# A layer of causal attention and soft mixture of experts in five stages: rows kept in SBUF for the slots stage, first inputs fetched a stage ahead, last stores awaited by their readers

## The reference, cut to what matters

```python
x = _layernorm(x + attention(x))          # causal, 16 heads of 32, 4 key/value groups
x = _layernorm(x + ffn(x))
# ffn, a soft mixture of E = 16 experts with S = 128 slots each:
x_ln = layernorm(x) * gamma + beta
x_n = l2norm(x_ln) * scale;  mu_n = l2norm(mu, 0)
logits = einsum('bnd,des->bnes', x_n, mu_n)
dispatch = softmax(logits, axis=1)                          # over tokens
combine = softmax(logits.reshape(B, N, E * S), axis=-1)     # over all slots
slot_in = einsum('bnd,bnes->besd', x_ln, dispatch)
slot_out = gelu(slot_in @ W1 + b1) @ W2 + b2
out = einsum('bsd,bns->bnd', slot_out, combine)
```

## Time and profile before

| what | value |
|---|---|
| time of the runs, median | 2615.83 us |
| time of the profiled execution | 2613.21 us |
| its span | 2611.5 us |
| granted TensorE clock, mean | 0.967 |
| PE busy | 2472.7 us, 95% |
| DVE busy | 1745.1 us, 67% |
| POOL busy | 1637.5 us, 63% |
| ACT busy | 1447.1 us, 55% |
| bytes moved by DMA | 337.98 MB |

### The profile page before, as it was taken

The page is one execution under the profiler, slowest core; times in us unless marked ns, Lnnn a source line. Parts: engine busy times, 40 slices in busy tenths (PEclk is TensorE's granted clock), DMA queues, the critical chain, the costliest instruction groups (busy, mean ns, idle before and its releaser), DMA issues. The chain is left out here.

```text
span 2611.5 us, 39531 instructions
## 1 busy us (share of the span) xinstructions
PE 2472.7 (95%) x13218; PEld 1725.6 (66%) x13218; DVE 1745.1 (67%) x3729; ACT 1447.1 (55%) x2780; POOL 1637.5 (63%) x1681
## 2 busy tenths in 40 slices
PE   8989999999999999996976999997999998799998
PEld 6865555555555555544755888886888886688886
DVE  3348887878787778744975565666665564577776
ACT  3214566666666666664874565566565563454553
POOL 4304868687776777786955766764767664355553
PEclk9978999999999999998988999998999998899999
DMA  7851121212112121104976454566444543875453
GB/s 241 287 154 37 35 60 39 64 33 66 46 51 61 46 50 49 39 9 145 348 257 163 151 161 129 163 201 177 147 153 134 163 143 109 297 229 144 138 156 102
DMA packets 237834, 337.98 MB, mean 129 GB/s; under 512 B 56608, under 2 KB 102720, under 8 KB 233408
## 3 DMA queue, kind: packets, MB, share of 16 engines
q1 hardware_dynamic: 201296, 294.72, 36.9%
q0 software_dynamic: 34688, 38.87, 5.1%
q10 hardware_dynamic: 1648, 1.88, 0.2%
HBM read 184.83 MB, written 116.42 MB: 115 GB/s over the span
## 5 line engine op out<-in xcount | busy, mean ns | idle before, releaser
L834 ACT ACTIVATE p_probs<-p_ps_s 128x512 f32<-128x512 f32 (+3 forms) x1280 | 596.8, 538 | 339.3 <-PE p_ps_s L766 329.5
L1360 POOL DMA_DIRECT2D p_eT<-p_ex x1024 | 538.6, 535 | 304.1 <-DVE p_ex L1624 252.2
L861 DVE TENSOR_REDUCE p_parts<-p_ps_m 128x1 f32<-128x512 f32 x768 | 472.1, 680 | 91.1 <-PE p_ps_m L753 90.8
L722 POOL TENSOR_TENSOR p_added<-p_added,p_probs 128x2048 f32<-128x2048 f32 x112 | 513.5, 4585 | 20.7 <-ACT p_probs L834 8.4
L753 PE MATMUL p_ps_m<-k_m,q 96*128 96x512 f32 (+3 forms) x1280 | 476.8, 403 | 13.0 <-PEq L1893 7.5
L766 PE MATMUL p_ps_s<-q,k_e 98*128 98x512 f32 (+3 forms) x1280 | 450.1, 381 | 2.2 <-ACT p_probs L834 2.2
L753 PEld LDWEIGHTS p_ps_m<-k_m,q 96*128 96x128 f32 x1280 | 242.6, 192 | 186.7 <-DVE p_parts L861 89.4
L766 PEld LDWEIGHTS p_ps_s<-q,k_e 98*128 98x128 f32 x1280 | 238.1, 190 | 135.1 <-issue 56.7
L785 PE MATMUL p_ps_c<-p_probs,v_e 128*32 128x512 f32 (+3 forms) x2560 | 287.5, 540 | 3.7 <-POOL p_probs L707 3.7
L865 DVE CUSTOM_DVE_ANT_0 p_masked<-p_ps_m,p_mask 128x384 f32<-128x384 f32 (+3 forms) x512 | 223.8, 487 | 98.8 <-PE p_ps_m L753 95.3
L1754 POOL TENSOR_TENSOR p_acc<-p_acc,p_lg 128x512 f32<-128x512 f32 x112 | 162.3, 1449 | 153.4 <-ACT p_lg L1806 150.4
(11 more groups left out here) (179 smaller groups left out, 4444.5 us busy)
## 6 DMA issues: line engine op xcount, KB each, us to landing
logits_t<-p_logit SPq DMA_DIRECT2D x32, 1024.0 KB, 5.0
p_eT<-p_ex POOLq DMA_DIRECT2D x1024, 32.0 KB, 2.0
p_lg<-logits_t SPq DMA_DIRECT2D x128, 256.0 KB, 3.7
q<-q_t SPq DMA_DIRECT2D x96, 256.0 KB, 4.6
p_w_raw<-L_ffn_W_dram SPq DMA_DIRECT2D x64, 256.0 KB, 5.4
p_so<-slot_out SPq DMA_DIRECT2D x32, 512.0 KB, 6.4
p_x<-L_attn_x_dram SPq DMA_DIRECT2D x32, 256.0 KB, 5.5
q_t<-p_f_hi SPq DMA_DIRECT2D x32, 256.0 KB, 5.4
```

The source lines that it names most:

```text
L722: pool.tensor_tensor(a[:, :, :], first[:, :, :], probs[s % RING][:, :, :], ALU.add).then_inc(s_add, 1)
L834: act.activation(probs[s % RING][:, h, q0:BLK], ps_s[:, u % ST_BANKS, q0:BLK], ACT.Exp).then_inc(s_exp, 1)
L861: dve.tensor_reduce(to, bank, AX.X, ALU.max).then_inc(s_taken, 1)
L1360: pool.dma_start(eT[r][p * QD:(p + 1) * QD, i, :, :], ex[i * QD:(i + 1) * QD, 2 * r:2 * r + 2, bass.ts(p, P)]).then_inc(s_eT[r], 16)
```

## The change

The change has these parts. (1) The waits for the last stores move from the ends of projections, post and slots into the next stage: to the start of SyncE's list there, or, for tiles that stay in SBUF, to the step that reads them. Attention's waits move into post, before its ninth pair of tiles; its stage end waits for a new load instead. The semaphores concerned outlive the barrier. (2) Wo is loaded and split in attention: ScalarE splits a quarter behind the first score of blocks 8 to 11, VectorE behind the first maximum of blocks 16 to 19. The first context tile is loaded at attention's end. The ones in k_e are set in projections. (3) post stores the unit rows and x_ln of batch 1 into SBUF tiles that the slots stage reads in place; only those of batch 0 go to DRAM. The first expert's mu is loaded too. Slots therefore takes batch 1 first. x_ln is no longer loaded by quarters but by tiles; to match, the logits' matmuls read the tokens of a group in another order (16 runs of 32 columns), and combine reads x1 and writes the output in that order. (4) The orders of ScalarE's and VectorE's parts in slots change: the splits of x_ln at the change of batch stand behind other parts and wait by tile, and the last quarter's split goes ahead of mu's split, the unit rows' splits and the copy of the slot output. SyncE's x_ln loads go ahead of the slot store. (5) At its end slots loads combine's first four logit tiles, the first largest logits and all slot outputs of its first batch; combine's tiles lie over those of slots.

```diff
                 store(blk)
-            for m in range(NF):
-                sp.wait_ge(s_ohi[m], 16 * NBLK)
-                sp.wait_ge(s_olo[m], 16 * NBLK)
-            for j in range(2):
-                sp.wait_ge(s_ov[j], 16 * NBLK // 2)
-            sp.wait_ge(s_first, 16 * 10 * QB)
...
+            dve.memset(first[2][QROWS:MROWS, :].bitcast(F32), 1.0).then_inc(s_rows, 1)
+            dve.wait_ge(s_rows, 1)
             split_lo(0)
...
+            for m in range(GROUPS + 1):
+                sp.wait_ge(s_ohi[m], 16 * NBLK)
+                sp.wait_ge(s_olo[m], 16 * NBLK)
+            for j in range(2):
+                sp.wait_ge(s_ov[j], 16 * NBLK // 2)
             sp.dma_start(mu_sq[:, :], d["mu_sq"]).then_inc(s_nin, 16)
+            sp.dma_start(w_raw[:, :, :], Wo.rearrange("(g p) c -> p g c", p=P)).then_inc(s_wo, 16)
...
+            sp.wait_ge(s_st[0], 16 * (2 * QB * GROUPS // 4))
+            sp.dma_start(c_first[:, :, :], d["ctx"][0, :, :, 0:2 * P].rearrange("g p n -> p g n")).then_inc(s_cin, 16)
             sp.wait_ge(s_nout, 16)
-            for r in range(2):
-                sp.wait_ge(s_st[r], 16 * NBK // 2)
+            sp.wait_ge(s_cin, 16)
...
             for what, a, h in order():
...
-                    if a == 0 and h == 0:
-                        pe.wait_ge(s_krow, 1)
...
+                    if h == 0 and a in WEIGHT_STEPS:
+                        g = WEIGHT_STEPS.index(a)
+                        act.wait_ge(s_wo, 16)
+                        act.activation(w_hi[:, g, :], w_raw[:, g, :], ACT.Copy).then_inc(s_whi, 1)
...
-            dve.memset(k_e[QROWS:MROWS, :].bitcast(F32), 1.0).then_inc(s_krow, 1)
...
                     maximum(a)
+                    if MAXU[a][0] in WEIGHT_BLOCKS and MAXU[a][1:] == (0, 0, 0):
+                        g = WEIGHT_BLOCKS.index(MAXU[a][0])
+                        dve.wait_ge(s_whi, g + 1)
+                        dve.tensor_tensor(w_lo[:, g, :], w_raw[:, g, :], w_hi[:, g, :], ALU.subtract).then_inc(s_wlo, 1)
...
+                if k == NT // 2:
+                    for half in range(2):
+                        sp.wait_ge(s_ctx_st[half], 16 * NBK // 2)
+                if k > 0:
+                    sp.dma_start(c_raw(k)[:, :, :], d["ctx"][b, :, :, bass.ds(m * 2 * P, 2 * P)].rearrange("g p n -> p g n")).then_inc(s_c[r], 16)
...
+                to = d["xl"][n] if n < NT else kept_xl[:, n - NT, :].bitcast(F32)
+                sp.dma_start(to, xl[n % R4][:, :]).then_inc(o_xl[n % R4], 16)
...
+                to = d["xT"][n] if n < NT else kept_xT[:, n - NT, :].rearrange("p (c t) -> p c t", c=DC).bitcast(F32)
+                sp.dma_start(to, xt[n % R4][:, :, :]).then_inc(o_t[n % R4], 16)
...
+                if i == TT:
+                    sp.dma_start(kept_mu[:, :, :], mu.rearrange("(c p) e s -> p e c s", p=P)[:, 0, :, :]).then_inc(s_kept, 16)
...
-            for r in range(R4):
-                for o in (o_x1, o_xl, o_t):
-                    sp.wait_ge(o[r], 16 * TT // R4)
+            sp.wait_ge(s_kept, 16)
...
-            for g in range(GROUPS):
-                act.dma_start(w_raw[:, g, :], Wo[bass.ts(g, P), :]).then_inc(s_w[g], 16)
...
-            for g in range(GROUPS):
-                act.wait_ge(s_w[g], 16)
-                act.activation(w_hi[:, g, :], w_raw[:, g, :], ACT.Copy).then_inc(s_whi, 1)
             act.wait_ge(s_scale, 16)
...
             def load_rows(j):
                 def part(n):
-                    if starts(n):
-                        if n > 0:
-                            sp.wait_ge(s_prod, 4 * n - JG + j + 1)
-                        for p in range(NQ):
-                            sp.dma_start(xl_lo[p * QD:(p + 1) * QD, j * TG:(j + 1) * TG, :].bitcast(F32),
-                                         d["xl"][n // E * NT + j * TG + p].rearrange("(t a) c -> a t c", a=QD)).then_inc(s_xl[j], 16)
+                    if starts(n) and n > 0:
+                        sp.wait_ge(s_prod, 4 * n - JG + j + 1)
+                        for t in tiles(j):
+                            sp.dma_start(xl_lo[:, t, :].bitcast(F32), d["xl"][t]).then_inc(s_xl[t], 16)
                 return part
...
+            def next_logits(n):
+
+                if n == UNITS - 1:
+                    sp.wait_ge(s_ex, 4 * UNITS)
+                    sp.wait_ge(s_most, 4 * UNITS)
+                    sp.wait_ge(o_l, 16 * UNITS)
+                    sp.wait_ge(o_m, 16)
+                    for k in range(4):
+                        sp.dma_start(logit[:, k, :], d["logit"][k, :, bass.ds(0, BLK)]).then_inc(s_next, 16)
+                    sp.dma_start(kept_top[:, :], d["top"][0, 0:TG, :].rearrange("t p -> (t p)").partition_broadcast(P)).then_inc(s_next, 16)
+
+            def next_slots(half):
+
+                def part(n):
+                    if n == UNITS - 1:
+                        sp.wait_ge(s_log, 4 * UNITS)
+                        sp.wait_ge(o_so, 32 * E)
+                        to = (kept_xT, kept_hi)[half]
+                        for e in range(E):
+                            sp.dma_start(to[:, e, :].bitcast(F32), d["so"][0, half, :, e, :]).then_inc(s_next, 16)
+                return part
+
+            for r in range(R4):
+                for o in (o_x1, o_xl, o_t):
+                    sp.wait_ge(o[r], 16 * TT_ALL // R4)
             walk([(0, load_mu)] + [(0, load_unit_rows(j)) for j in range(JG)]
-                 + [(1, store_logits)] + [(2, load_weights)] + [(3, store_out)] + [(1, load_rows(j)) for j in range(JG)])
-            sp.wait_ge(o_l, 16 * UNITS)
-            sp.wait_ge(o_so, 32 * UNITS)
-            sp.wait_ge(o_m, 16 * B)
+                 + [(1, store_logits)] + [(2, load_weights)] + [(1, load_rows(j)) for j in range(JG)] + [(3, store_out)]
+                 + [(1, next_slots(0)), (2, next_logits), (2, next_slots(1))])
+            sp.wait_ge(s_next, 16 * (2 * E + 5))
...
                         mm = three_passes(pe, ps_l[:, j, :], m_hi[r][:, c, :], m_lo[r][:, c, :],
-                                          xT_hi[:, group(j), c, :], xT_lo[:, group(j), c, :], c == 0, c == DC - 1)
+                                          by_block(xT_hi[:, group(j), c, :]), by_block(xT_lo[:, group(j), c, :]), c == 0, c == DC - 1)
...
-                            act.wait_ge(s_xT[t], n // E * 16 + 16)
+                            if n > 0:
+                                act.wait_ge(s_xT[t], 16)
+                            else:
+                                act.wait_ge(o_t[t % R4], 16 * ((NT + t) // R4 + 1))
...
             def rows_hi(j, first):
                 def part(n):
                     if starts(n) and (n == 0) == first:
-                        act.wait_ge(s_xl[j], n // E * 64 + 64)
                         for t in tiles(j):
+                            if n > 0:
+                                act.wait_ge(s_xl[t], 16)
+                            else:
+                                act.wait_ge(o_xl[t % R4], 16 * ((NT + t) // R4 + 1))
                             act.activation(xl_hi[:, t, :], xl_lo[:, t, :].bitcast(F32), ACT.Copy).then_inc(s_xlhi, 1)
...
-            walk([(3, slot_in), (2, rows_hi(0, False)), (1, copy(0)), (2, rows_hi(1, False)), (3, slot_in_hi), (1, copy(1)), (2, split_hi(0)),
-                  (2, rows_hi(2, False)), (1, copy(2)), (3, gelu), (2, rows_hi(3, False)),
-                  (2, split_hi(1)), (1, copy(3)), (1, exp(0)), (1, exp(1)), (2, split_hi(2)), (1, exp(2)), (1, exp(3)),
-                  (0, vectors_hi), (0, unit_rows_hi(0)), (0, unit_rows_hi(1)), (3, out_hi), (2, split_hi(3)),
+            walk([(3, slot_in), (1, copy(0)), (3, slot_in_hi), (1, copy(1)), (2, split_hi(0)), (2, rows_hi(0, False)),
+                  (1, copy(2)), (3, gelu), (2, rows_hi(1, False)), (2, split_hi(1)), (1, copy(3)), (2, rows_hi(2, False)), (1, exp(0)), (1, exp(1)),
+                  (2, split_hi(2)), (2, rows_hi(3, False)), (1, exp(2)), (1, exp(3)), (2, split_hi(3)),
+                  (0, vectors_hi), (0, unit_rows_hi(0)), (0, unit_rows_hi(1)), (3, out_hi),
                   (0, unit_rows_hi(2)), (0, unit_rows_hi(3))]
                  + [(1, rows_hi(j, True)) for j in range(JG)] + [(2, weights_hi), (2, largest_row)])
...
-            walk([(3, slot_in_lo), (2, rows_lo(0, False)), (1, maximum(0)), (1, largest(0)), (2, rows_lo(1, False)), (1, maximum(1)), (2, split_lo(0)), (1, largest(1)),
-                  (2, rows_lo(2, False)), (1, maximum(2)), (3, hidden_lo), (2, rows_lo(3, False)), (2, split_lo(1)), (1, maximum(3)), (3, bias),
-                  (1, largest(2)), (1, turn(0)), (1, turn(1)), (2, split_lo(2)), (1, turn(2)), (1, turn(3)), (0, vectors_lo), (0, unit_rows_lo(0)),
-                  (1, largest(3)), (0, unit_rows_lo(1)), (1, total), (3, out_lo), (2, split_lo(3)), (1, largest_col), (0, unit_rows_lo(2)), (0, unit_rows_lo(3))]
+            walk([(3, slot_in_lo), (1, maximum(0)), (1, largest(0)), (1, maximum(1)), (2, split_lo(0)), (1, largest(1)), (2, rows_lo(0, False)),
```

(39 more changed lines are left out.)

140 lines of the change are left out of this document (81 added, 59 removed).

## The result

The changed kernel takes 2639.3 us (median of 4 runs, 2638.98 to 2639.45) against 2616.4 for the kernel before on the same chip (2615.61 to 2619.16): ratio 1.0085, interval 1.0068 to 1.0103. It is 23 us slower; 2573.9 was forecast, 42 us faster. The profiled execution has a span of 2637.5 us against 2611.5.

A forecast was written before the change was run, and what follows sets the result against it. TensorE's path was taken to set the end, with non-matmul time in seven gaps. Terms 2.5 - 1.0 + 1.1 + 1.9 + 16.5 + 13.9 + 7.0 = 41.9 us off 2615.8 gave 2573.9; range 2567 to 2582 (0.62), wider 2563 to 2592.

The forecast's parts named there:

- Loads and stores stay 2 KB per row: nothing.: Logits, x1 and output change token order in runs of 32; claimed to cost nothing.
- Rival (b): Slots stage: logits' moving operand in 16 runs of 32 reads dearer, kernel slower; 50 ns more each gives 2651; chance 0.05.
- Attention itself: Attention: Wo's split adds eight instructions of 0.7 us, mostly hidden; 1.0 us lost, bounds 0 and 5.6.
- Projections to attention: Attention's start: TensorE enters earlier, the load of the squares is late next; gain 2.5 us, bounds 0 and 5.5.
- Attention to post: Post's start: Wo's wait gone, but exit later for the first context tile's load; gain 1.1 us, bounds -2.6 and 4.
- Post to slots: Slots' start: earlier exit, rows already in SBUF; gain 1.9 us, bounds 0 and 3.
- First two units: Slots' start: the 14.5 us gap and its low-clock restart go, rows being in place; gain 16.5 us, bounds 12 and 18.5.
- Change of batch: Slots: last quarter's split goes first, gain 3.1; rows' unit 28.8 us, not 39.6, gain 10.8; together 13.9, bounds 8 and 18.
- Slots to combine: Combine's start: 5.5 MB of end loads are the new wait, but everything is in place; gain 7.0 us, bounds -0.3 and 10.4.
- Rival (a): Slots' gaps are refilled by other work in units 0 and 16, end loads slow; gain 24.5, 2591 us; chance 0.22.
- (c): Two waits left at the change of batch go too and end loads are hidden; gain 49.3, 2566.5 us; chance 0.09.

The follow-up runs named there:

- with only the second mended: Changed kernel with VectorE's four subtractions for Wo's low part in attention replaced by one-input operations (output wrong): 2625.7 us, ratio 1.0051.
- with only the first mended: Changed kernel with combine's x1 loads and output stores again 128 consecutive rows, logits' columns reordered at c_hi, c_lo and the running sum: 2580.0 us, ratio 0.9862.
- whole tiles: Changed kernel with combine's x1 loads and output stores again as tiles of 128 consecutive rows: 2580.0 us, ratio 0.9862.
- both losses mended: Changed kernel with 128-consecutive-row x1 loads and output stores in combine, and attention's four Wo low-part subtractions moved from VectorE to GpSimd: 2567.9 us, ratio 0.9820.
- with the rows turned: Changed kernel with 128-row combine transfers and GpSimd doing Wo's subtractions, logits' columns in old contiguous order, kept x_ln rows laid by blocks of 32: 2571.8 us, 0.9836.

## Why the prediction was wrong

Two of its steps failed. The first alone takes the time out of the range and makes the kernel slower: with only the second mended it is 2625.7 us. The second alone does neither: with only the first mended it is 2580.0, inside 2563 to 2592.

**"Loads and stores stay 2 KB per row: nothing."** This sentence of the sum is the main failure. I looked at the size of a piece, which indeed stays, and not at how a transfer is spread over the engines. It cost 61.5 us where it was made alone, and mending it gave back 59; the table shows 52.3, most likely because the new place of combine's weights hides some 9 of it. Rival (b) priced the new order of tokens as well, but on TensorE's side; no rival stood on the DMA's.

**"Attention itself".** I took 0.7 us for each of Wo's four low parts, from a VectorE row at a quiet place, with 5.6 us as the bound for all eight instructions. The step lost 13.1 us in the trace, and 12.1 came back when it was mended beside whole tiles. The trace of before held the warning. In its combine stage GpSimd adds beside VectorE in pieces of 1.4 us (L1754), and this line's group shows (min, median, max ns):

```profile
L1842 DVE TENSOR_TENSOR p_c_lo<-p_lg,p_c_hi x128: 675/684/1764, 2232.8 to 2589.5; 128x512 fp32r<-128x512 f32 x128
```

Its longest is 1.1 us over the median, less than one such addition. In attention GpSimd's additions are of 4.59 us (L722, 112 of them), and VectorE's maxima, which read at most one input from SBUF, are not held by them. Four times up to 4.6 us, with the restart of TensorE behind each, was the bound to write. It was partly luck that only two of the four met an addition.

**The steps that held.** Projections to attention: 2.9 for 2.5, and the squares' matmuls wait for their load at 175.3 as said. Attention to post: about nothing for 1.1; TensorE's gap is 14.29 against 14.22 us. Post to slots: 4.8 for 1.9, beyond its bound of 3; 3.0 are the shorter wait of the first logits (8.99 against 11.99), and 1.8 lie inside post (0.4 with both losses mended); their cause stays open. First two units: 15.1 for 16.5, inside 12 to 18.5, and the gap of 14.5 is gone (with both losses mended it is 2.25 and the stretch gains 12.5). Change of batch: the unit of the rows takes 29.8 us for the forecast 28.8, of 39.6; from the first to the last closed unit the stage is 789.2 - 772.9 = 16.4 us shorter for 13.9, of which 12.6 lie in the three units there; steady units, 0.19 us shorter each, give 5.1, and the last two take 1.3 more. Slots to combine: 25.0 - 19.8 = 5.1 for 7.0, from the last closed unit to combine's first matmul (its lower bound, 7.0 - 7.7, is -0.7 and not -0.3). The end loads are the new wait, as forecast. They are all issued ahead of the last store, but land behind it: the DMA share stays near 1 until 2202, and SyncE waits for them until 2202.4.

```profile
2186.08 8.60 SPq L1372 DMA_DIRECT2D xT_hi<-slot_out  x16
...
2197.87 0.32 SPq L1351 DMA_DIRECT2D slot_out<-p_so_lo  x1
```

```profile
SPq L1245 <- DMA xT_hi<-slot_out: 4.2, 1, 4.2
```

```profile
2200.00:2202.00 2.00, 0.00 (x0) 0.00 (x0) 0.00 (x0) 0.00 (x0) 0.00 (x0) 0.50 1.02 384
```

They end 4.5 us behind the last store's issue where the forecast had 3.1 (2221.5 - 2218.42); that is 1.4 of the 1.9 us missing.

**Rival (b)** has the right sign and a small size. The moving operand in 16 runs of 32 costs 5 ns a matmul; logits groups from 1420 to 1700 (busy, mean ns), first of the changed kernel, with runs of 32, then with the rows turned, contiguous:

```profile
L75 PE MATMUL p_ps_l<-xT_hi,w_o_lo 128*128 128x512 f32 x185 | 73.2, 396 | 0.0
```

```profile
L75 PE MATMUL p_ps_l<-xT_hi,w_o_lo 128*128 128x512 f32 x187 | 73.1, 391 | 0.0
```

That is 24.58 - 24.33 = 0.25 us for a unit and 8 us for 32. The new order of the lists (25.02 to 24.58) more than hides it, so the unit looked untouched by it: 24.59 against 24.8. The prediction's sentence by which (b) was out does not cover these 5 ns. Rival (a) did not come, and neither did (c).

With both failures mended the time is 2567.9 us, 6 below the forecast. That closeness is partly luck: 9.7 us come from combine, which no step had and which the place of its weights (10.4 us where moved in the kernel before) can account for; without them it would be some 4 above.

## What to carry to other kernels

When a rearranged view enters a transfer, count the entries of its slowest dimension before counting bytes: with 4 of them, 128 rows of 2 KB went at 100 GB/s here, and the loads on the same queue came late. Before an operation moves to an engine that "has room", look at what runs beside it there, and read the longest duration of its group, not the mean: 0.68 us became 4.88 beside GpSimd's additions. A stage in which "nothing changes" deserves a row of its own in the sum; here both such stages decided the result.

## What was not expected of the hardware

The same matmuls follow each other every 219 or every 226 ns (183 and 177 in 40 us) after an edit that only orders allocations, most likely by where their weights lie in SBUF: 10.4 us of 2614. And behind one gap of 4.05 us, with TensorE busy without a break from 640 until it, the granted clock was 0.50 from 655 to 665, so the restart cost up to 5 us more (an estimate: half of that stretch).
